# Image attention of a four-layer Flamingo kernel: output products in odd steps, the gathered keys' exponentials on ScalarE, routing's sends in every second step

## The chip, the core and the metric

The program runs on one core of one Trainium2 chip. The metric is the device time of one execution in microseconds (us), lower is better. Engines are called by the profile's names: PE is TensorE (its weight loads are PEld), DVE is VectorE, ACT is ScalarE, POOL is GpSimd, SP is the queue that issues the hardware DMAs.

## What is computed

Four layers work on `x` (4 batches of 512 tokens, 128 wide). Each adds a gated cross-attention and a gated feed-forward block. The change touches the first attention and the first steps of the routing that follows it. Cut to that, the reference is:

```python
def _L0_xattn_ref(image_embeds, latents, ln1_g, ln1_b, ln2_g, ln2_b, Wq, Wkv, Wo):
    x = layer_norm(image_embeds, ln1_g, ln1_b)       # ctx_1024: 4 x 154 x 128
    l = layer_norm(latents, ln2_g, ln2_b)            # layernorm(x): 4 x 512 x 128
    q = l @ Wq
    kv = jnp.concatenate([x, l], axis=1) @ Wkv       # 666 keys
    k, v = jnp.split(kv, 2, axis=-1)                 # 16 heads of 64
    w = softmax(q k^T / 8)                           # 4 x 16 x 512 x 666
    out = w @ v
    return out @ Wo

def _L0_ffn_ref(x, gate_w, gate_b, expert_bias, w1, b1, w2, b2):
    top_idx = jnp.argmax(x @ gate_w.T + gate_b + expert_bias, axis=-1)   # 8 experts
    ...

x = x + tanh(g_xattn[0]) * _L0_xattn_ref(ctx_1024, _layernorm(x), ...)
x = x + tanh(g_ffn[0]) * _L0_ffn_ref(_layernorm(x), ...)
```

## The kernel before

Every engine has its own program, written out by hand, and waits on semaphores where it needs another. Nothing is scheduled by a tool: the order in which an engine's function issues is the order in which it runs. The first attention (`image_pe`, `image_ve`, `image_ac`, `image_po`, `image_sp`) is a loop of 271 steps `i` that all engines walk through. The first 256 each start one piece of 128 queries of one head with all 666 keys. Four of them make a unit (two heads, two query tiles), two units a group (a pair of heads), and eight groups (64 steps) a batch.

What one step `i` issues, with the lines that the trace shows:

- **PE**: scores of step `i` (four products, L715) into one of two pairs of PSUM banks; in even steps a part of the product with the values of the unit before last (L749, 18 or 12 products, and in one of the two also L755 and the transposes L647); the transposes of the probabilities of step `i-2` (four on L726 into bank 4, the fifth on L730 into bank 5); where `i % 4 == 3` one more transpose of `rest` (L733); then, in even steps, a part of the projections of the next group (L495) into bank 7, called `side`.
- **DVE**: the maximum of step `i` over 666 scores (L787); in odd steps the low half of the projection of the step before (L860, L868, or L872 and L875, by part), which frees bank 7; the copy of the fifth tile out of bank 5 (L801); where `i % 4 == 3` also the product of a finished unit with its inverse sums (L783, at the step's start) and two instructions on `rest` (L808, L809), of which the second frees bank 5.
- **ACT**: the copy of the four transposed tiles of step `i-2` (L901), then the exponential of step `i` out of PSUM with its row sum (L911, 128x666, followed by the read of the accumulator), then every fourth step L920, and in even steps the high half of the projection (L943, L949, L955, L957).
- **POOL**: the low halves of the transposed probabilities of step `i-3` (two instructions on L1028); every fourth step L998 and L1006; and a copy of 32 columns (L1034, semaphore mark `gathered`): the last 32 of the 666 keys of step `i-1` go from `probs` into `rest`, where the four pieces of a unit stand side by side, to be transposed together by PE (L733). PE waits for the copies, and the exponential of step `i` waits for the copy of step `i-3`, because it overwrites that buffer. From step 32 on POOL also splits weights of the next layer in every fourth step (L1061, L1062, L1065).

Three things are placed by step numbers. `image_late` says in which steps PE multiplies a finished batch's `mixed` by `Wo`: four steps in a row, each with one tile of 128 tokens and 24 products of 128x128 (L495, `out<-in` named `banks<-weights_a,work`), followed by DVE's addition to `x` (L844). These products use bank 7 too (for the last batch banks 7 and 4), and wait until `mixed_low`, POOL's L1006, has passed the batch's last unit. `image_chores` says where the routing of the next layer starts: at step 222 its logits, at 225 its ranks, and from 227 on twelve `send`s, each an indirect DMA issued by POOL (L1185). `rest_due` says when `rest` is transposed.

The bank that PE takes is guarded by `bank`: it waits for the event that last freed it. For bank 7 in a late step that is DVE's low half of the projection issued one or more steps earlier; for a projection after a late product it is L844.

## Time and profile before

| what | value |
| --- | --- |
| time, median of 3 runs (lowest to highest) | 1881.87 us (1881.65 to 1882.85) |
| the profiled execution: its own time | 1886.16 us |
| the profiled execution: span | 1884.3 us |
| PE busy | 1471.7 us (78%) |
| DVE busy | 1181.1 us (63%) |
| ACT busy | 808.0 us (43%) |
| POOL busy | 780.4 us (41%) |
| chain that ended last, by engine | PE 52%, DVE 25%, ACT 7%, issue 7%, POOL 5%, DMA 3% |

The image attention lies between about 36 and 687 us of the span. The profiled execution took 4.3 us more than the median; the 1.9 us between its time and its span lie outside the traced program. A busy share is an average over the eight parts of the program, so what a step costs has to be read in the stretch in which it lies.

### The profile page before, as it was taken

The numbers are of one execution on the slowest core, as the hardware profiler recorded it, in microseconds if no ns is written. First come the engines' busy times: TensorE is split into PE (matmuls) and PEld (weight loads), VectorE is DVE, ScalarE is ACT, GpSimd is POOL, SyncE is SP. The second block draws the span as 40 slices with busy tenths as digits, with TensorE's granted clock in tenths as the row PEclk, the third lists the DMA queues.
The fourth block names the chain that finished last, engine by engine and source line by source line (L and its number), as shares of the span: only waits on it lengthen the run. The fifth ranks groups of instructions, "written<-read, shape, count | busy, mean of one in ns | idle before, by whom it ended". The sixth has DMA issues, their size and how long they took to land.

```text
span 1884.3 us, 32544 instructions
## 1 busy us (share of the span) xinstructions
PE 1471.7 (78%) x11363; PEld 955.5 (51%) x11485; DVE 1181.1 (63%) x3053; ACT 808.0 (43%) x1838; POOL 780.4 (41%) x1240
## 2 busy tenths in 40 slices
PE   4899899999989859463288689958966885578877
PEld 2666666667766648351265345523442333335444
DVE  4777577667766636438938656554566556776643
ACT  3777677767766626210044245533212542111011
POOL 4789798888767944400012333000002101243220
PEclk9999999999999989756568799979996977788887
DMA  6323222112112113300000000000000000000000
GB/s 246 90 80 108 67 71 53 43 39 54 45 42 54 50 47 101 115 0 0 1 0 1 11 5 1 2 1 1 1 1 1 1 1 1 0 1 6 5 2 11
DMA packets 35446, 63.96 MB, mean 34 GB/s; under 512 B 7527, under 2 KB 25026, under 8 KB 34131
## 3 DMA queue, kind: packets, MB, share of 16 engines
q1 hardware_dynamic: 33815, 59.77, 10.6%
q0 software_dynamic: 1472, 2.12, 0.3%
q8 instruction: 94, 1.54, 0.3%
q14 instruction: 65, 0.53, 0.1%
HBM read 30.59 MB, written 12.66 MB: 23 GB/s over the span
## 4 chain that ended last, share of the span: by engine, by line
PE 52%; DVE 25%; ACT 7%; issue 7%; POOL 5%; DMA 3%; SPq 0%; ACTq 0%; DVEq 0%; POOLq 0%
PE banks L495 13%; PE banks L715 4%; PE banks L749 4%; PE banks L1955 4%; PE banks L726 3%; ACT work L911 2%; DMA work<-work 2%; DVE xn L441 2%; PE banks L1941 2%; PE banks L1867 1%; PE banks L470 1%; DVE norm_room L405 1%; PE banks L1908 1%; POOL work L1028 1%; PE banks L2647 1%
## 5 line engine op out<-in xcount | busy, mean ns | idle before, releaser
L1028 POOL TENSOR_TENSOR work<-work 128x512 bf16<-128x512 f32 (+1 forms) x512 | 358.8, 724 | 96.4 <-ACT work L901 94.1
L435 POOL TENSOR_TENSOR norm_room<-norm_room,minus_half 128x4 f32<-128x4 f32 x48 | 50.1, 1045 | 537.3 <-DVE norm_room L410 535.4
L787 DVE TENSOR_REDUCE work<-banks 128x1 f32<-128x666 f32 x256 | 216.0, 844 | 50.8 <-PE banks L715 50.4
L911 ACT ACTIVATE work<-banks,work 128x666 f32<-128x666 f32 x256 | 209.1, 817 | 50.2 <-DVE work L787 42.7
L901 ACT ACTIVATE work<-banks 128x512 f32<-128x512 f32 x256 | 154.1, 602 | 131.4 <-PE banks L726 130.1
L715 PE MATMUL banks<-work 128*128 128x154 bf16 (+1 forms) x932 | 171.7, 299 | 28.2 <-DMA work<-work 17.9
L495 PE MATMUL banks<-work,weights_b 128*128 128x512 bf16 (+1 forms) x830 | 159.5, 350 | 12.6 <-DVE work L2282 5.1
L726 PE MATMUL banks<-const,work 128*128 128x128 f32 x1024 | 158.0, 277 | 2.2 <-ACT work L901 2.2
L715 PEld LDWEIGHTS banks<-work 128*128 128x128 bf16 x1024 | 91.7, 98 | 109.2 <-DMA work<-work 22.2
L476 ACT ACTIVATE xt<-banks 128x512 f32<-128x512 f32 x48 | 28.7, 598 | 264.0 <-PE banks L470 264.0
L470 PE MATMUL banks<-const,xn 128*128 128x128 f32 x176 | 39.8, 367 | 130.4 <-DVE xn L441 84.0
L749 PE MATMUL banks<-work 128*64 128x256 bf16 x1920 | 133.8, 279 | 7.1 <-POOL work L1028 5.3
L2032 DVE TENSOR_REDUCE work<-banks 128x2 f32<-128x308 f32 x192 | 86.6, 474 | 72.0 <-PE banks L1913 39.3
L495 PEld LDWEIGHTS banks<-work,weights_b 128*128 128x128 bf16 (+1 forms) x840 | 83.7, 101 | 84.4 <-issue 20.5
L2854 POOL TENSOR_TENSOR work<-work 128x512 bf16<-128x512 f32 x64 | 67.6, 1060 | 139.4 <-DVE work L2803 139.4
L726 PEld LDWEIGHTS banks<-const,work 128*128 128x128 f32 x1024 | 111.9, 141 | 16.6 <-issue 15.1
L749 PEld LDWEIGHTS banks<-work 128*64 128x64 bf16 x1920 | 97.3, 108 | 24.8 <-POOL work L1028 8.0
L2011 ACT ACTIVATE work<-banks 128x256 f32<-128x256 f32 (+1 forms) x256 | 85.6, 382 | 56.2 <-PE banks L1944 36.2
L470 PEld LDWEIGHTS banks<-const,xn 128*128 128x128 f32 x176 | 26.2, 184 | 143.4 <-DVE xn L441 77.8
L801 DVE COPY work<-banks 128x128 f32<-128x128 f32 x256 | 72.3, 282 | 39.2 <-PE banks L730 37.9
L730 PE MATMUL banks<-const,work 128*128 128x128 f32 x256 | 73.1, 285 | 8.1 <-ACT xt L478 2.9
L1941 PE MATMUL banks<-work 128*128 128x256 bf16 (+1 forms) x256 | 64.7, 287 | 14.6 <-ACT work L2003 11.6
(416 smaller groups left out, 3317.0 us busy)
## 6 DMA issues: line engine op xcount, KB each, us to landing
work<-work SPq DMA_DIRECT2D x128, 166.5 KB, 3.0
sorted<-in_pads SPq DMA_DIRECT2D x10, 838.5 KB
weights_b<-in_weights SPq DMA_DIRECT2D x1, 4120.0 KB, 23.9
work<-scratch SPq DMA_DIRECT2D x64, 64.0 KB, 2.0
weights_b<-in_weights SPq DMA_DIRECT2D x1, 2824.0 KB, 9.6
weights_a<-in_weights SPq DMA_DIRECT2D x1, 2056.0 KB, 9.1
weights_a<-in_weights SPq DMA_DIRECT2D x1, 2050.0 KB, 10.0
work<-work SPq DMA_DIRECT2D x32, 64.0 KB, 1.9
```

What stands on the lines that cost most here:

```text
L470: i = pe.transpose(ps[:, j * P:j * P + rows], src[0:rows, j, :], self.eye[0:rows, 0:rows])
L495: m = pe.matmul(out, left(a), right(b), start=start and n == 0, stop=stop and n == 2)
L715: m = pe.matmul(slot[:, a:z], lhs, k[:, h, part, a:z], start=part == 0, stop=part == 1)
L726: m = pe.transpose(ps[:, t * P:(t + 1) * P], prob[:, t * P:(t + 1) * P], self.eye)
L749: pe.matmul(self.out_bank[64 * h:64 * h + 64, 0:2 * P], self.v[n % 3][:, t, of_values, 64 * h:64 * h + 64], self.probs_parts[u % 2][:, h, ...
L787: ve.tensor_reduce(self.neg_max[i % 4], self.slot[i % 2][:, 0:KEYS0], AX_X, ALU.max, negate=True).then_inc(self.mark("max"))
L901: ac.activation(self.probs_t[u % 2][:, h, 0:4, j * P:(j + 1) * P], self.bank_a.rearrange("p (t n) -> p t n", t=4), ACT.Copy).then_inc(self ...
L911: ac.activation(self.probs[i % 3], self.slot[i % 2][:, 0:KEYS0], ACT.Exp, bias=self.neg_max[i % 4], accum_out=self.sums[u % 4][:, 2 * j + ...
L1028: po.tensor_tensor(parts[:, :, :, 0], exact, parts[:, :, :, 1], ALU.subtract).then_inc(self.mark(event, i - 3))
L1941: m = pe.matmul(bank, left, a.q4[b % 2][:, g, cols], start=True, stop=s != 4)
L2011: ac.activation(out, self.bank_of(k, HALF)[0:rows_n, :], ACT.Exp).then_inc(self.mark("exp4", s, n))
L2032: ve.tensor_reduce(a.most[u % 2][:, c % 2, 2 * g:2 * g + 2], self.bank_of(n % 3, 2 * CTX).rearrange("p (h k) -> p h k", h=2), AX_X, ALU.ma ...
```

## The change

Three edits, all within the first attention:

1. `image_late`: the four products with `Wo` of a batch stood in steps 73, 74, 75, 76 (and 64, 128, 192 later). They now stand in 69, 71, 73, 75. The first two wait for one unit less of `mixed_low`.
2. `gathered` is gone. POOL no longer copies 32 columns per step; instead ACT computes the exponentials of these 32 scores a second time, straight from PSUM into `rest`, ahead of the exponential of all 666. The wait of the exponential on the copy goes too, and PE's transpose of `rest` waits for `exp`.
3. `send`s stand in steps 227, 229, ..., 249 in place of 227 to 238.

```diff
-        elif 5 <= route < 5 + ROUTED:
-            out.append(("send", route - 5, 0))
+        elif route in range(5, 5 + 2 * ROUTED, 2):
+            out.append(("send", (route - 5) // 2, 0))
...
-        late = i - 8 * PAIRS - 9
-        if late >= 0 and late % (8 * PAIRS) < QT:
-            return late // (8 * PAIRS), late % (8 * PAIRS)
+        late = i - 8 * PAIRS - 5
+        if late >= 0 and late % (8 * PAIRS) in range(0, 2 * QT, 2):
+            return late // (8 * PAIRS), late % (8 * PAIRS) // 2
...
-                pe.wait_ge(*self.at("mixed_low", 2 * PAIRS * (b + 1)))
+                pe.wait_ge(*self.at("mixed_low", 2 * PAIRS * (b + 1) - int(t < 2)))
...
-            pe.wait_ge(*self.at("gathered", 4 * rest + 3))
+            pe.wait_ge(*self.at("exp", 4 * rest + 4))
...
-                    ac.wait_ge(*self.at("gathered", i - 3))
...
+                at = 32 * (2 * j + h)
+                ac.activation(self.rest[u % 2][:, at:at + 32], self.slot[i % 2][:, KEYS0 - 32:KEYS0], ACT.Exp, bias=self.neg_max[i % 4])
...
-            if 1 <= i < SUBS + 1:
-                u, _, _, _, h, j = self.image_sub(i - 1)
-                if (h, j) == (0, 0) and u >= 2:
-                    po.wait_ge(*self.at("turned_b", 4 * u - 2))
-                po.wait_ge(*self.at("exp", i))
-                po.tensor_copy(self.rest[u % 2][:, 32 * (2 * j + h):32 * (2 * j + h + 1)], self.probs[(i - 1) % 3][:, KEYS0 - 32:]).then_inc(self.mark("gathered", i - 1))
```

**On PE, the first batch's second late product, before** (step 74; `x24` on `weights_a,work` is the product with `Wo`, L715 the scores, L749 the values, L726 and L730 the transposes). It comes right behind the transposes of its own step, and a projection follows it:

```order
L715 MATMUL banks<-work 128x512 x2
L715 MATMUL banks<-work 128x154 x2
L749 MATMUL banks<-work 64x256 x12
L755 MATMUL banks<-work 128x128 x6
L647 MATMUL banks<-const,work 128x128 x2
L726 MATMUL banks<-const,work 128x128 x4
L730 MATMUL banks<-const,work 128x128
L495 MATMUL banks<-weights_a,work 128x128 x24
L495 MATMUL banks<-weights_c,weights_a 128x512 x2
L495 MATMUL banks<-weights_c 128x512
```

**The same product now** (step 71), with the end of step 70 ahead of it:

```order
L495 MATMUL banks<-weights_a,weights_c 128x128 x2
L495 MATMUL banks<-weights_c 128x128
L495 MATMUL banks<-weights_a,weights_c 128x128
L715 MATMUL banks<-work 128x512 x2
L715 MATMUL banks<-work 128x154 x2
L726 MATMUL banks<-const,work 128x128 x4
L730 MATMUL banks<-const,work 128x128
L733 MATMUL banks<-const,work 128x128
L495 MATMUL banks<-weights_a,work 128x128 x24
```

Between the projection of step 70 and the late product of step 71 PE now has only one short step: its scores and six transposes. No projection follows within the step.

**On ACT, one step now** (L901 the copy of step `i-2`, L911 the new exponential, L912 the old one; L921 and L950 are L920 and L949 of before):

```order
L901 ACTIVATE work<-banks 128x4x128
L911 ACTIVATE work<-banks,work 128x32
L912 ACTIVATE work<-banks,work 128x666
L921 ACTIVATE work<-banks 128x256
L950 ACTIVATE work<-banks 128x512
```

The 128x32 row is new in every step, between the copy and the exponential.

**On POOL, from the copy that ends step 226 to the transposed tiles of step 228, before** (L1185 is the send, L1034 the copy of 32 columns):

```order
L1034 COPY work<-work 128x32
L1185 DMA sorted<-xn,places 16640x129
L1028 TENSOR_TENSOR work<-work 128x4x128
L1028 TENSOR_TENSOR work<-work 128x128
L1034 COPY work<-work 128x32
L998 COPY work<-work 128x256
L1006 TENSOR_TENSOR work<-work 128x256
L1185 DMA sorted<-xn,places 16640x129
L1028 TENSOR_TENSOR work<-work 128x4x128
L1028 TENSOR_TENSOR work<-work 128x128
```

**The same place now**, from the send of step 227 to that of step 229 (the send is L1180, L1029 is L1028 of before, L999 and L1007 are L998 and L1006):

```order
L1180 DMA sorted<-xn,places 16640x129
L1029 TENSOR_TENSOR work<-work 128x4x128
L1029 TENSOR_TENSOR work<-work 128x128
L999 COPY work<-work 128x256
L1007 TENSOR_TENSOR work<-work 128x256
L1029 TENSOR_TENSOR work<-work 128x4x128
L1029 TENSOR_TENSOR work<-work 128x128
L1180 DMA sorted<-xn,places 16640x129
```

Two steps' work stands between two sends, and the copies are gone.

## Rows read from the trace of the kernel before

**Rows 1.** Busy time by stretch: us from:to, length, busy (x instructions) by engine, PEclk, DMA.

```profile
453.19:470.95 17.76, 17.50 (x179) 13.03 (x181) 12.89 (x31) 14.05 (x35) 14.15 (x29) 1.00 0.20 52
293.51:313.45 19.94, 17.90 (x179) 12.99 (x181) 14.97 (x39) 14.24 (x35) 18.76 (x34) 1.00 0.18 45
```

**Rows 2.** Timeline of one unit: start us, us, engine, line, what [idle before <-releaser].

```profile
455.57 0.60 PE L726 MATMUL banks<-const,work 128*128 128x128 f32 x4
...
456.27 0.60 ACT L901 ACTIVATE work<-banks 128x512 f32<-128x512 f32 x1 [1.18 <-PE banks L726]
...
456.76 0.81 ACT L911 ACTIVATE work<-banks,work 128x666 f32<-128x666 f32 x1
...
457.56 0.38 ACT L920 ACTIVATE work<-banks 128x256 f32<-128x256 f32 x1
...
457.97 0.42 DVE L783 TENSOR_TENSOR work<-banks,work 128x256 f32<-128x256 f32 x1 [1.29 <-ACT work L920]
457.99 0.73 PE L715 MATMUL banks<-work 128*128 128x512 bf16 x4
...
458.31 0.84 DVE L787 TENSOR_REDUCE work<-banks 128x1 f32<-128x666 f32 x1
...
459.07 0.68 DVE L872 TENSOR_TENSOR work<-banks,work 128x512 bf16<-128x512 f32 x1
...
460.18 0.30 DVE L809 TENSOR_TENSOR work<-banks,work 128x128 bf16<-128x128 f32 x1
...
460.54 0.33 PE L730 MATMUL banks<-const,work 128*128 128x128 f32 x1
```

**Rows 3.** Waits of PE's weight loads, 36 to 687 us: us in total, times, longest us.

```profile
PEld banks L730 <- DVE work L809: 13.4, 42, 0.4
```

**Rows 4.** ACT's short exponentials, groups by shape (1700 to 1884 us): busy us, mean ns | idle.

```profile
L2721 ACT ACTIVATE work<-banks,work 128x512 f32<-128x512 f32 x3 | 2.1, 687 | 5.9 <-DVE work L2825 5.9
...
L2721 ACT ACTIVATE work<-banks,work 128x128 f32<-128x128 f32 x3 | 1.1, 368 | 8.2 <-DVE work L2825 8.2
```

**Rows 5.** PE's waits around the late products of the third batch, 505 to 547 us.

```profile
PE banks L495 <- DVE x L844: 1.2, 2, 0.8
PE banks L495 <- DVE scratch L868: 1.1, 1, 1.1
PE banks L715 <- DMA work<-work: 1.1, 1, 1.1
PE banks L495 <- DVE work L872: 1.0, 1, 1.0
```

**Rows 6.** Timeline behind a part-2 projection, where step 69 now has its late product.

```profile
462.36 0.73 PE L715 MATMUL banks<-work 128*128 128x512 bf16 x4
...
463.32 0.80 DVE L875 TENSOR_TENSOR work<-banks,work 122x128 bf16<-122x128 f32 x3
```

**Rows 7.** PE's waits for POOL where the sends stand, 599 to 641 us.

```profile
PE banks L749 <- POOL work L1028: 5.3, 2, 2.9
```

**Rows 8.** Busy time by stretch, right behind the longer of these two waits.

```profile
635.00:640.00 5.00, 5.00 (x35) 3.47 (x36) 0.62 (x2) 1.88 (x4) 5.00 (x11) 0.66 0.00 0
```

**Rows 9.** Timeline of POOL between two sends.

```profile
606.30 1.00 POOL L1185 DMA_INDIRECT sorted<-xn,places  x1 [0.17 <-ACT work L911]
...
607.33 1.41 POOL L1028 TENSOR_TENSOR work<-work 128x512 bf16<-128x512 f32 x2
...
608.66 0.21 POOL L1034 COPY work<-work 128x32 f32<-128x32 f32 x1
...
609.04 1.00 POOL L1185 DMA_INDIRECT sorted<-xn,places  x1 [0.17 <-issue]
```

**Rows 10.** Timeline of the tail, where the last batch's late products stand.

```profile
677.05 1.92 PE L749 MATMUL banks<-work 128*64 128x256 bf16 x30 [0.98 <-DVE work L783]
...
680.66 0.61 POOL L1006 TENSOR_TENSOR work<-work 128x256 bf16<-128x256 f32 x1 [3.06 <-DVE work L783]
681.33 5.68 PE L495 MATMUL banks<-weights_a,work 128*128 128x128 bf16 x96 [1.69 <-POOL work L1006]
```

**Rows 11.** ACT's waits, 36 to 687 us.

```profile
ACT work L911 <- POOL work L1006: 2.6, 7, 0.4
ACT work L911 <- POOL work L1028: 1.8, 5, 0.4
ACT work L911 <- POOL work L1034: 1.1, 3, 0.6
```

More of the change, by code:

```diff
@@ L190 @@
         "clear": "filled", "tokens": "filled", "four_times": "filled", "wo_low": "filled", "mixed_low": "low_b", "summed": "router_steps", "ranked": "routed",
-        "places": "placed", "tile_stats": "ve", "gathered": "low_b", "padded": "router_steps", "relative": "router_steps", "delta": "router_steps",
+        "places": "placed", "tile_stats": "ve", "padded": "router_steps", "relative": "router_steps", "delta": "router_steps",
         "mix": "router_steps", "gates": "gate_steps", "gate_exp": "gate_steps"}
```

## The prediction

> **What bounds the kernel now.** All three edits lie in the first attention (36 to 687 us), so I read that stretch alone, in this order: busy time by stretch, to find the engine that is full; the timeline of one unit of four steps, to see what is waited for; PE's waits by releaser, to see how often; then the three places where the steps are moved.
>
> In an undisturbed group (eight steps) PE is busy for 17.50 of 17.76 us [rows 1]. That reads as "PE is the bound", but the timeline shows how thin this is. The reader should follow one unit from PE's transposes of an even step: they start at 455.57 and are issued by 456.01 (four, 0.11 us apart). ACT copies them from 456.27, starts the exponential at 456.76, and L920 at 457.56; DVE multiplies with that from 457.97, takes the next maximum at 458.31, the low half of the projection at 459.07, and then L809 at 460.18, which frees bank 5. PE's fifth transpose waits for it and starts at 460.54 [rows 2]. PE had issued the four transposes ahead of it by about 460.23, so it lost some 0.3 us. This loop is closed once per unit, from transposes to transposes, and it ends last: PE's weight load on L730 waits for L809 in 42 of 64 units, 13.4 us in all [rows 3]. So PE and a chain ACT, DVE, PE run level, with the chain 0.3 us behind. Whatever lengthens that chain is paid in full; ACT's and POOL's shares (14.05 and 14.15 of 17.76 us, rows 1) say nothing on it. **The exponential stands in the chain, POOL doesn't.**
>
> **The change part by part.**
>
> *The second exponential on ACT.* 256 instructions of 128x32 are added, each between the copy (L901) and the exponential (L911), so in each unit one of them is in the chain. No row shows this shape. The nearest are exponentials out of PSUM with a bias from SBUF, as this one: 128x512 takes 687 ns, 128x128 takes 368 ns [rows 4], so 0.83 ns a column, and 32 columns would take 0.29 us. Instructions of ACT overlap: the copy of 0.60 us starts at 456.27 and the exponential behind it at 456.76 [rows 2], 0.11 us before its end. So each new one delays the next by 0.29 - 0.11 = 0.18 us. The bounds: 0.29 if it doesn't overlap; below, 0.06, if the bias cost nothing and the fixed part were hidden; nothing at all if the chain weren't the bound (a rival). I take 0.18. How often: all 64 units close the chain or a longer one that holds the exponential too (through the projection's copies, the DMA of the keys and the next scores); I leave out four for the start, so 60 x 0.18 = **+10.8 us**, with 3.6 and 17.4 as ends.
>
> The Trainium skill (ScalarE: Activation LUTs, section "What ACT_TABLE_LOAD costs") states 280 ns + 0.833 ns a column for an ACTIVATE with a pointer as bias, and an overlap of 93 ns between neighbours. By it the new instruction would take an estimated 307 ns and delay the next by 0.21 us, and the change's sum would be 1.8 us higher; for the two shapes in rows 4 it gives 0.71 and 0.39 us where the trace has 0.687 and 0.368, so I stay with the rows.
>
> *The copies taken from POOL.* 256 x 0.21 us [rows 9] go. Outside the sends nothing waits for POOL except in name (see the rivals), so they bring nothing there; the work that remains (L1028) is what PE needs, two steps after it is ready. Counted with the sends below.
>
> *The products with Wo.* The 24 products themselves are unchanged, four times in each batch. What changes is the wait for bank 7. Before, in each of the first three batches, PE waits 1.1 us for L868 and 1.0 us for L872 ahead of the odd ones (73, 75), and 1.2 us in two waits for L844, since a projection stands right behind the even ones; the third batch also shows 1.1 us for the DMA of the keys at the start of the group ahead [rows 5], and so does the first (same row, 190 to 232 us), but not the second. Now each product stands in an odd step, one short step behind the projection of the even step whose low half has to free the bank:
> - steps 71 and 75 (`i % 4 == 3`): the chain above up to the end of L872 is 459.07 + 0.68 = 459.75, with 0.1 us to PE 459.85. PE would be ready when it starts the next scores, at 457.99 [rows 2]. That is 1.86 us each, and since the chain starts at the transposes of the step before, the stall of an earlier late product doesn't shorten it.
> - step 69: L875 ends at 464.12 and PE is ready at 462.36 [rows 6], so 1.86 us with the same 0.1.
> - step 73: as before, 1.1 us [rows 5].
>
> Sum 6.7 us against 3.3, or 4.4 with the DMA wait, which the stalls at 69 and 71 now cover. In the second batch one wait of 0.3 us for L809 goes too. So +2.3, +3.1 and +2.3: **+7.7 us**. As bounds I take 0 (as many stalls as before) and +10 (the DMA waits stay).
>
> *The sends.* One costs POOL 1.00 us and 0.17 ahead of it, and from one to the next it takes 609.04 - 606.30 = 2.74 us [rows 9], against 2.22 us per step elsewhere (17.76 / 8, rows 1). Over 12 steps POOL falls behind until PE waits for L1028, 5.3 us in two waits [rows 7]; behind the longer one PE's granted clock is 0.66 over 5 us [rows 8], between its levels of 1.2 and 2.4 GHz, which I put at 0.34 x 5 = 1.7 us. Now 24 steps hold the sends: eight steps of POOL cost 14.15 - 8 x 0.21 + 4 x 1.17 = 17.2 us, less than the 17.8 to 18.1 that the others take. So both go, less 0.6 us for what the chain would take anyway: **-6.4 us**. Ends: -3 and -8.
>
> *The tail.* The last batch's 96 products start at 681.33, when L1006 (680.66) is done, and take 5.68 us; PE had been idle for 1.69 us [rows 10]. Two of the four may now start before the last unit is finished: one between L749's 18 and 12 products of 677.05, one behind its transposes. They fill the idle time and leave some 0.4 us of waiting for L1006: **-1.3 us**. Ends: -2 and 0.
>
> The sum is 10.8 + 7.7 - 6.4 - 1.3 = **+10.8 us**. The profiled execution would go from 1886.16 us (span 1884.3) to 1897.0, and the median of the runs, 4.3 us below it, from 1881.87 to **1892.7 us**, 0.57% slower.
>
> **The rivals.**
>
> *POOL sets the pace in the groups with weight splits; the change is faster.* In such a group POOL is busy for 18.76 of 19.94 us and the group takes 2.2 us longer than the undisturbed one [rows 1], and the trace names POOL as what released 15 exponentials, 5.5 us in all [rows 11]. If the copies on POOL held such a group up, 8 x 0.21 = 1.7 us of each would go. There are 16 groups with splits (steps 32 to 160); I take half of them to be like the one shown, -13 us, with the exponential paid only in the others (+5.4) and the moved steps cancelling (+7.7 - 7.7): -8 in all, 1874 us (1860 if all 16 gain). It decides for faster once the gain over all groups passes 9.2 us, 0.6 us for each of the 16. For it: the two rows. Against it: PE's waits name POOL in the sends alone, and at most of those releases ACT's own copy had ended only just before, so the copy on POOL is a tie rather than the cause. Chance 0.14.
>
> *The odd steps cost nothing.* If DVE's low halves come earlier than in the undisturbed group, the waits of the late products stay as they are and the sum is 10.8 - 7.7 = +3.1: 1885 us, within 0.2% or just over. For it: before, the waits ahead of 73 and 75 are only 1.1 and 1.0 us. Against: 75 profits there from the late product of 74, which lay in the chain's shadow and no longer does. Chance 0.15.
>
> *The chain has room.* If PE's own 17.50 us are the bound, the second exponential disappears in the 0.3 us: 7.7 - 7.7 = 0, 1882 us. Rows 3 speak against it: a wait that shows in 42 units is no room. Chance 0.12.
>
> *The sends still hold POOL up*, now over 24 steps, because it waits for ACT's copies in between: +10.8 + 6.4 = +17, 1899 us. Chance 0.07. My forecast has the remaining 0.52.
>
> **How the numbers follow.** About 0.2% (3.8 us) is what a measurement of this kernel can tell from no change. Slower by more: the forecast and the last rival, most of the half in which sizes differ, and a third of the "odd steps" case: 0.65. Within: most of "odd steps" and of "the chain has room": 0.19. Faster: the POOL case and the rest: 0.16. The range: 1892.7 with the ends of the exponential (-7, +7) and of the late products (-8, +2) gives 1880 to 1901; to leave out no more than 2 in 10 I go to 1879 and 1902, which takes in the rivals but the first. The forecast's own range is 1886 to 1901.
>
> **What would show it.** In the new profile: the 128x32 rows at about 0.29 us and the main exponential starting 0.18 us after them; an undisturbed group of 18.1 us in place of 17.76; PE's waits on L730 longer than 0.3 us, about 0.5; four waits of PE before each batch's products with Wo, three near 1.9 us and one of 1.1, and none for L844; no wait of PE for L1028 (now L1029) between steps 227 and 250, and a granted clock of 1.0 there; no idle time ahead of the last products. I am wrong if groups keep 17.76 us, or if groups with splits get shorter.

## The result, and the profile after

| | before | changed |
| --- | --- | --- |
| median of 4 runs (lowest to highest), us | 1882.36 (1881.65 to 1887.31) | 1915.45 (1908.32 to 1917.57) |
| the profiled execution, time and span, us | 1886.16, 1884.3 | 1917.49, 1915.7 |

The changed kernel is slower, ratio 1.0158 (95% interval 1.013 to 1.0186). The forecast was 1892.7 us with a range of 1879 to 1902: right in sign, a third of the size. Of the 31.4 us between the two profiled spans, 22.2 lie in the image attention (its last addition L844 ends at 687.40 before, 709.63 now), 9.2 in what follows.

The page of the changed kernel, engine totals and two groups (L911 is now the new exponential, L912 the old one; the lines from there to POOL's L1029, which is L1028 of before, are one further):

```profile
PE 1504.4 (79%) x11485; PEld 966.0 (50%) x11485; DVE 1187.1 (62%) x3053; ACT 851.0 (44%) x2094; POOL 742.7 (39%) x984
...
L749 PE MATMUL banks<-work 128*64 128x256 bf16 x1920 | 136.7, 282 | 2.1 <-DVE work L783 1.8
...
L730 PE MATMUL banks<-const,work 128*128 128x128 f32 x256 | 72.7, 284 | 13.4 <-DVE work L809 7.4
```

ACT gained 256 instructions (2094, before 1838), POOL lost 256 (984, before 1240), and the waits on POOL ahead of L749 [rows 7] are gone. Busy time by stretch: first the undisturbed group, then the group with splits of rows 1 and steps 225 to 249, in which the sends stand.

```profile
472.87:491.22 18.35, 18.02 (x182) 13.01 (x181) 12.95 (x31) 15.45 (x42) 12.95 (x21) 1.00 0.20 51
```

```profile
304.67:324.51 19.84, 17.99 (x182) 13.02 (x181) 14.79 (x40) 15.65 (x42) 17.15 (x26) 1.00 0.18 46
622.24:679.46 57.22, 53.63 (x549) 38.92 (x547) 40.03 (x98) 45.59 (x123) 50.32 (x72) 1.00 0.23 61
```

The undisturbed group takes 18.35 us where it took 17.76 [rows 1]; the one with splits 19.84 against 19.94, so the prediction's last sign of being wrong, a shorter group with splits, shows in this one (e10 and e11 below take it up). ACT's groups by shape, over the attention:

```profile
L912 ACT ACTIVATE work<-banks,work 128x666 f32<-128x666 f32 x256 | 209.7, 819 | 0.0
...
L911 ACT ACTIVATE work<-banks,work 128x32 f32<-128x32 f32 x256 | 73.9, 289 | 47.5 <-DVE work L787 46.9
```

One unit of the undisturbed group, the same instructions as in rows 2, and what follows them up to the next unit's transposes:

```profile
475.36 0.60 PE L726 MATMUL banks<-const,work 128*128 128x128 f32 x4
...
476.06 0.60 ACT L901 ACTIVATE work<-banks 128x512 f32<-128x512 f32 x1 [0.94 <-PE banks L726]
...
476.55 0.28 ACT L911 ACTIVATE work<-banks,work 128x32 f32<-128x32 f32 x1
...
476.72 0.82 ACT L912 ACTIVATE work<-banks,work 128x666 f32<-128x666 f32 x1
...
477.51 0.39 ACT L921 ACTIVATE work<-banks 128x256 f32<-128x256 f32 x1
...
477.94 0.42 DVE L783 TENSOR_TENSOR work<-banks,work 128x256 f32<-128x256 f32 x1 [1.47 <-ACT work L921]
```

```profile
480.15 0.31 DVE L809 TENSOR_TENSOR work<-banks,work 128x128 bf16<-128x128 f32 x1
480.36 0.84 DVE L787 TENSOR_REDUCE work<-banks 128x1 f32<-128x666 f32 x1
...
480.51 0.33 PE L730 MATMUL banks<-const,work 128*128 128x128 f32 x1 [0.19 <-DVE work L809]
...
481.31 0.29 ACT L911 ACTIVATE work<-banks,work 128x32 f32<-128x32 f32 x1 [0.30 <-DVE work L787]
481.50 0.81 ACT L912 ACTIVATE work<-banks,work 128x666 f32<-128x666 f32 x1
...
482.45 0.54 PEld L715 LDWEIGHTS banks<-work 128*128 128x128 bf16 x4 [0.19 <-ACT work L912]
482.45 0.74 PE L715 MATMUL banks<-work 128*128 128x512 bf16 x4
...
484.50 0.49 PE L726 MATMUL banks<-const,work 128*128 128x128 f32 x3
```

The same two places of before, behind its L730 at 460.54 (its next scores start at 462.36 [rows 6], and no wait for ACT stands ahead of them):

```profile
461.35 0.82 ACT L911 ACTIVATE work<-banks,work 128x666 f32<-128x666 f32 x1 [0.21 <-DVE work L787]
...
464.40 0.49 PE L726 MATMUL banks<-const,work 128*128 128x128 f32 x3
```

The reader should see two passages through the new exponential, not one. From L726 to L730 it is 480.51 - 475.36 = 5.15 us, before 460.54 - 455.57 = 4.97 [rows 2]: that is the chain of the prediction, +0.18. But from L730 on there is a second one: DVE's maximum, the new exponential (481.31), the old one (481.50, ends 482.31), and only then the bank is free for the scores at 482.45. That part, up to the next unit's L726, takes 3.99 us; before it was 464.40 - 460.54 = 3.86, so +0.13. Over the whole attention PE's weight loads of the scores wait for the exponential 31 times where they waited 13 times (first before, then the changed kernel: us in total, times, longest):

```profile
PEld banks L715 <- ACT work L911: 6.1, 13, 0.7
```

```profile
PEld banks L715 <- ACT work L912: 10.5, 31, 0.9
```

PE's waits in the 16 steps of the third batch's late products:

```profile
PE banks L495 <- DVE work L872: 1.9, 1, 1.9
PE banks L495 <- DVE work L875: 1.9, 1, 1.9
PE banks L495 <- DVE work L860: 1.9, 1, 1.9
PE banks L495 <- DVE scratch L868: 1.2, 1, 1.2
```

That is as forecast. What was not forecast stands in the last number but two, the granted clock, of busy time by stretch (first batch, 2.5 us each):

```profile
203.38:205.88 2.50, 1.72 (x22) 1.24 (x19) 1.53 (x4) 2.15 (x9) 1.97 (x3) 1.00 0.00 0
205.88:208.38 2.50, 1.39 (x24) 1.42 (x25) 1.23 (x5) 1.50 (x4) 1.40 (x2) 0.98 0.39 91
208.38:210.88 2.50, 2.50 (x19) 1.38 (x16) 1.29 (x3) 0.00 (x0) 0.00 (x0) 0.50 1.23 354
210.88:213.38 2.50, 2.50 (x31) 2.17 (x27) 0.29 (x1) 0.75 (x3) 0.07 (x1) 0.83 0.43 178
```

The first of the four waits ends at 206.99. Within 1.5 us of it the clock is at 0.50, the lower of PE's levels (1.2 GHz), and stays there for some 3 us. It happens once more in this batch, behind the last of the four waits, which ends at 231.2. The 16 steps of each batch as a whole:

```profile
194.25:247.20 52.95, 44.59 (x458) 33.28 (x457) 28.84 (x70) 31.18 (x83) 31.18 (x46) 0.94 0.22 67
```

```profile
363.83:415.44 51.61, 43.11 (x458) 32.42 (x457) 28.82 (x70) 31.35 (x83) 31.23 (x46) 0.97 0.14 36
```

```profile
527.93:578.16 50.23, 42.98 (x458) 32.47 (x457) 28.71 (x70) 30.53 (x83) 25.98 (x41) 0.97 0.14 36
```

Before, these took 46.59, 45.76 and 45.41 us, at 1.00.

The clock also falls in places that the change did not make. At step 222, while PE runs the 24 thin products of the routing's logits (128x8), it goes to 0.50 for 3.4 or 6.8 us in 12 of the 17 profiles of this document, before (587.6) and changed (614.5) among them. Such a fall costs time in whichever profile happens to have it, so sums of profiles carry it as noise.

Last the tail, PE's timeline (rows 10 of before):

```profile
701.59 1.56 PE L495 MATMUL banks<-weights_a,work 128*128 128x128 bf16 x24
...
704.46 1.54 PE L495 MATMUL banks<-weights_a,work 128*128 128x128 bf16 x24
706.32 2.93 PE L495 MATMUL banks<-weights_a,work 128*128 128x128 bf16 x48 [0.31 <-POOL work L1007]
```

Two of the four products did move into the idle time ahead of L1007.

### The profile page after: what moved, and what is told of

Read it like the earlier page. It is cut to its first block, busy times and chain, and to the rows that moved or that the text cites. A ratio compares the mean times of both kernels' runs of the same rounds, so it can differ in the third digit from the quotient of the medians.

```text
span 1915.7 us, 32544 instructions
## 1 busy us (share of the span) xinstructions
PE 1504.4 (79%) x11485; PEld 966.0 (50%) x11485; DVE 1187.1 (62%) x3053; ACT 851.0 (44%) x2094; POOL 742.7 (39%) x984
## 4 chain that ended last, share of the span: by engine, by line
PE 52%; DVE 26%; ACT 10%; issue 6%; DMA 3%; POOL 2%; SPq 0%; ACTq 0%; DVEq 0%; POOLq 0%
PE banks L495 12%; ACT work L912 4%; PE banks L749 4%; PE banks L715 4%; PE banks L1950 4%; PE banks L726 3%; DMA work<-work 2%; DVE xn L441 2%; PE banks L1936 2%; PE banks L1862 2%; PE banks L470 1%; DVE work L787 1%; PE banks L1903 1%; DVE norm_room L405 1%; PE banks L755 1%
## 5 line engine op out<-in xcount | busy, mean ns | idle before, releaser
L1029 POOL TENSOR_TENSOR work<-work 128x512 bf16<-128x512 f32 (+1 forms) x512 | 357.7, 723 | 161.0 <-ACT work L901 159.4
L787 DVE TENSOR_REDUCE work<-banks 128x1 f32<-128x666 f32 x256 | 216.0, 844 | 45.5 <-PE banks L715 44.7
L912 ACT ACTIVATE work<-banks,work 128x666 f32<-128x666 f32 x256 | 209.7, 819 | 0.0
L901 ACT ACTIVATE work<-banks 128x512 f32<-128x512 f32 x256 | 155.0, 605 | 117.9 <-PE banks L726 112.6
L715 PE MATMUL banks<-work 128*128 128x512 bf16 (+1 forms) x1024 | 190.7, 309 | 20.3 <-DMA work<-work 12.8
L726 PE MATMUL banks<-const,work 128*128 128x128 f32 x1024 | 157.4, 276 | 2.4 <-ACT work L901 2.3
L715 PEld LDWEIGHTS banks<-work 128*128 128x128 bf16 x1024 | 90.3, 98 | 113.2 <-DMA work<-work 16.7
L749 PE MATMUL banks<-work 128*64 128x256 bf16 x1920 | 136.7, 282 | 2.1 <-DVE work L783 1.8
L726 PEld LDWEIGHTS banks<-const,work 128*128 128x128 f32 x1024 | 111.5, 141 | 16.7 <-issue 15.6
L749 PEld LDWEIGHTS banks<-work 128*64 128x64 bf16 x1920 | 100.3, 110 | 21.7 <-issue 6.5
L911 ACT ACTIVATE work<-banks,work 128x32 f32<-128x32 f32 x256 | 73.9, 289 | 47.5 <-DVE work L787 46.9
L730 PE MATMUL banks<-const,work 128*128 128x128 f32 x256 | 72.7, 284 | 13.4 <-DVE work L809 7.4
```

The lines of the kernel that those rows point to most:

```text
L715: m = pe.matmul(slot[:, a:z], lhs, k[:, h, part, a:z], start=part == 0, stop=part == 1)
L726: m = pe.transpose(ps[:, t * P:(t + 1) * P], prob[:, t * P:(t + 1) * P], self.eye)
L749: pe.matmul(self.out_bank[64 * h:64 * h + 64, 0:2 * P], self.v[n % 3][:, t, of_values, 64 * h:64 * h + 64], self.probs_parts[u % 2][:, h, ...
L787: ve.tensor_reduce(self.neg_max[i % 4], self.slot[i % 2][:, 0:KEYS0], AX_X, ALU.max, negate=True).then_inc(self.mark("max"))
L901: ac.activation(self.probs_t[u % 2][:, h, 0:4, j * P:(j + 1) * P], self.bank_a.rearrange("p (t n) -> p t n", t=4), ACT.Copy).then_inc(self ...
L912: ac.activation(self.probs[i % 3], self.slot[i % 2][:, 0:KEYS0], ACT.Exp, bias=self.neg_max[i % 4], accum_out=self.sums[u % 4][:, 2 * j + ...
```

## The experiments

The table gives what each profiled execution shows, in us: the length of stretches between the starts of DVE's maxima (L787) of two steps, the granted clock in parentheses where it isn't 1.00; the end of the attention; and the span behind it, where all kernels run the same code. Each run's ratio is to executions of before that were taken beside it; their medians lie between 1883.8 and 1890.0 us (1890.0 for e9 to e12), so times of different runs should be compared by their ratios.

| kernel | 65-81 | 129-145 | 193-209 | 161-193 | 225-249 | end | behind |
| --- | --- | --- | --- | --- | --- | --- | --- |
| before | 46.59 | 45.76 | 45.41 | 71.08 | 61.53 (0.97) | 687.40 | 1196.9 |
| changed | 52.95 (0.94) | 51.61 (0.97) | 50.23 (0.97) | 73.42 | 57.22 | 709.63 | 1206.1 |
| e5_after_again | 51.44 (0.97) | 49.99 | 50.21 (0.97) | 73.60 | 57.12 | 710.16 | 1196.4 |
| e1_exp_only | 47.47 | 46.60 | 45.97 | 73.48 | 60.52 (0.97) | 700.03 | 1201.1 |
| e9_exp_behind | 47.11 | 46.19 | 45.61 | 72.27 | 58.61 | 690.83 | 1210.5 |
| e10_exp_added | 47.50 | 46.66 | 46.52 | 73.42 | 61.59 (0.97) | 701.25 | 1204.5 |
| e11_no_copies | 46.76 | 45.64 | 45.24 | 71.02 | 61.19 (0.97) | 689.13 | 1206.6 |
| e2_late_odd_only | 48.57 | 48.72 | 47.43 | 71.06 | 62.81 (0.97) | 695.68 | 1190.5 |
| e14_odd_again | 48.62 | 48.61 | 47.44 | 71.07 | 60.03 (0.97) | 695.96 | 1201.9 |
| e6_exp_and_odd | 51.44 (0.97) | 53.05 (0.94) | 48.64 | 73.56 | 60.59 (0.97) | 711.89 | 1192.6 |
| e15_odd_exp_local | 51.27 (0.97) | 49.85 | 50.17 (0.97) | 71.04 | 61.64 (0.94) | 701.01 | 1197.2 |
| e13_behind_odd_sends | 49.14 | 49.35 | 47.92 | 72.28 | 56.29 | 695.80 | 1191.8 |
| e12_exp_two_odd | 47.68 | 47.77 | 47.97 (0.96) | 73.42 | 58.94 | 700.62 | 1196.4 |
| e4_late_even_only | 44.30 | 44.37 | 43.11 | 71.06 | 62.55 | 681.73 | 1204.9 |
| e7_exp_and_even | 44.97 | 44.99 | 43.69 | 73.42 | 60.32 (0.97) | 693.50 | 1196.8 |
| e3_sends_only | 46.71 | 45.74 | 45.45 | 71.05 | 55.84 | 680.91 | 1196.7 |
| e8_even_and_sends | 44.32 | 44.23 | 43.07 | 71.06 | 55.55 | 674.21 | 1204.9 |

The last column spreads from 1190.5 to 1210.5 us, and between two executions of the changed kernel by 9.7 us. So the edits are weighed by where the attention ends, and the times of the runs stand beside them. Each row is one profiled execution.

### Each edit alone

**e1_exp_only**: the second exponential, POOL's copies gone (cut, against before).

```diff
-                    ac.wait_ge(*self.at("gathered", i - 3))
+                ac.activation(self.rest[u % 2][:, at:at + 32], self.slot[i % 2][:, KEYS0 - 32:KEYS0], ACT.Exp, bias=self.neg_max[i % 4])
```

> Only the second exponential on ACT in place of POOL's copy; late products and sends stand as before. Theory A (two passes): each unit of four steps holds the added 0.17 us twice, once ahead of L783 and once ahead of the next scores, so an undisturbed group goes from 17.77 to 18.36 us and the attention ends about 17 to 19 us later than before, less 1 us because POOL is a little lighter in the sends: 1898 to 1901 us if what comes after the attention keeps its time. Theory B (one pass, as forecast): 18.1 us a group, +10.8, 1893 us. Theory C (the loss of the changed kernel needs the parts together): under +5 us here.

1900.81 us, ratio 1.0076 (1.0049 to 1.0103). The attention ends 12.6 us later. Theory A is right for undisturbed groups (steps 161 to 193 are four of them, 73.48 / 4 = 18.37 us) and too high in the sum (17 to 19 us): elsewhere a unit pays less.

**e2_late_odd_only**: the four products in odd steps (the `image_late` edit and the wait on one unit less).

> Only the products with Wo moved to odd steps. Theory A: PE waits three times 1.7 us (1.9 less the 0.17 of the added exponential) and once 1.1 us ahead of them in each batch, and its granted clock falls below 1.0 right behind some of them, as in the changed kernel (0.83 and 0.72 over 5 us); 16 steps (65 to 81) take 3.5 to 5 us more than before in each of three batches, the tail gains 1.3 us: +10 to +12 us, 1892 to 1894 us. Theory B (waits alone, as forecast): +7.7 - 1.3, 1888 us. Theory C (the odd steps cost nothing): under +2 us.

1889.12 us, ratio 1.002 (0.9997 to 1.0043); the attention ends 8.3 us later, at a full clock in the three batches. Theory A missed: the waits are 1.7, 1.7, 1.1 and 1.7 us as it said, but no fall stands behind them.

**e3_sends_only**: the `send` edit.

> Only the sends in every second step; POOL keeps its 32-column copies. Theory A: PE's waits for L1028 (5.3 us) go and the clock stays at 1.0 between 590 and 660 us, -6 us, 1876 us; POOL needs 14.15 + 4 x 1.17 = 18.8 us for eight steps that take 17.8, so it falls behind by 1 us a group and its slack of some 3 us just holds. Theory B (POOL without the copies removed is still too slow): a wait of PE for L1028 remains near step 249, -2 to -4 us.

1879.82 us, ratio 0.9986 (0.9956 to 1.0016): too small for the runs to tell, but the attention ends 6.5 us earlier. Of these, 5.7 lie in steps 225 to 249; 0.8 lie in steps 209 to 225, where this profile happens to have no fall of the clock at step 222.

The three alone sum to 12.6 + 8.3 - 6.5 = 14.4 us. Together they cost 22.2. So 7.8 us belong to no edit alone.

**e4_late_even_only**: even steps in place of odd (against e2_late_odd_only).

```diff
-        late = i - 8 * PAIRS - 5
+        late = i - 8 * PAIRS - 6
```

> Only the products with Wo moved, to even steps (70, 72, 74, 76 and 64, 128, 192 later), ahead of the projection of the same step. Theory A: what makes an odd step dear is that PE reaches bank 7 only one short step behind the projection, while in an even step two steps have passed and the product fills the time of the chain: no wait for DVE's low halves, only four waits of 0.5 to 0.8 us for L844; 16 steps take 0.5 to 2 us less than before in each of three batches, the tail gains about 1 us: 1876 to 1880 us. Theory B (every spread costs, since it stalls four steps in place of a run of four): +3 us or more, as the odd steps do.

1882.63 us, ratio 0.9984 (0.9962 to 1.0005); the attention ends 5.7 us *earlier* than before. At these products and the projections behind them PE waits for L844 alone, four times in a batch, 0.5 to 0.8 us each. What costs is the odd step, one step behind the projection, not the earlier place or the distance.

### What only the combination costs

> The changed kernel once more, on the chip that runs the next three. Its first attention ended at 709.6 us in the first profile, where the sum of the three edits made alone gives 687.4 + 12.6 + 8.3 - 6.5 = 701.8. Theory A (the 7.8 us are an interaction of the edits): it ends at 709 to 710 again, and steps 65 to 81 take 52.5 to 53.5 us again. Theory B (the 7.8 us were this one execution): it ends near 702, steps 65 to 81 take near 50 us. What comes behind the attention is the same code in both kernels; if the 9 us by which it was longer than before belong to the change, it takes 1204 us or more again, if they are the spread of runs, anything from 1190 to 1206.

1910.41 us, ratio 1.0153 (1.013 to 1.0176). The attention ends at 710.16, so a loss beyond the sum comes back, 8.3 us, but it isn't the same one. Against the sum of the three edits made alone, the three times 16 steps hold 7.6 us of it in the first profile and only 4.5 here, where the clock falls in two of three batches and steps 65 to 81 take 51.44 us, between the two theories. Another 3.0 us of e5's lie in steps 209 to 225, where the fall at step 222 lasts 6.8 us; kernels without the combination show that as well (e7, e11, e14), and e1 and e3 have no fall there, which makes the sum too low. What follows the attention takes 1196.4 us here, as before the change.

**e6_exp_and_odd** (sends as before) and **e7_exp_and_even**:

> The second exponential and the products with Wo in odd steps, the sends as before. Theory A (the interaction is between these two: only both together lower TensorE's granted clock in the 16 steps of the late products): the attention ends at 709.6 + 6.5 = 716, steps 65 to 81 take about 53 us, granted clock there below 1.00. Theory B (they only add): 687.4 + 12.6 + 8.3 = 708.3, steps 65 to 81 take 46.6 + 0.9 + 2.0 = 49.5 us at a granted clock of 1.00.

> The second exponential, with the products with Wo in the four even steps 6, 8, 10, 12 behind the group's start (that alone ended the attention 5.7 us earlier than before) in place of the odd ones; sends as before. Theory A (the clock falls in the long waits ahead of the odd products, four of 1.1 to 1.9 us in 8 steps, once the exponential is there too): with even steps these waits are short, the edits add, the attention ends at 687.4 + 12.6 - 5.7 = 694 (693 to 696), clock 1.00 in steps 65 to 81. Theory B (the second exponential makes late products cost more wherever they stand): 700 or later.

e6: 1917.62 us, ratio 1.0188 (1.0164 to 1.0211), attention ends at 711.9: above the plain sum of 708.3, below the 716 of theory A. e7: 1894.21 us, ratio 1.0073 (1.0046 to 1.01), 693.5 us, and full clock in the three batches: the exponential and even products simply add (687.4 + 12.6 - 5.7 = 694.3). So the extra cost lies between the exponential and the *odd* products. It doesn't need the sends: e6 has it in the three times 16 steps, 6.1 us beyond the sum, though less in the whole attention (3.6), since its steps 81 to 129 and 225 to 249 are some 1.5 and 1.2 us shorter than the sum.

It has two parts. Where the clock held, both edits together made the 16 steps 49.99 (e5) and 48.64 us (e6) long, against 49.56 and 47.99 by adding e1's and e2's gains to before: 0.4 and 0.7 us, some 1.6 us over three batches, if the first is as long at full clock as the second. The rest is the clock: each 0.03 below 1.00 goes with about 1.5 us more (50.21 against 48.64, 51.61 against 49.99), and the profiled changed kernel has four such falls, some 6 us.

**e12_exp_two_odd**: two of the four in odd steps, two in even ones (offsets 5, 7, 10, 12).

> The second exponential, with two of the four products in odd steps (5 and 7 behind the group's start) and two in even ones (10 and 12); sends as before. Theory A (TensorE's granted clock falls behind the row of four long waits ahead of the odd products): with two such waits it stays 1.00 in the 16 steps of all three batches, which then take the mean of the even version (44.97, 44.99, 43.69) and of the odd one at full clock (49.99, 49.99, 48.64): 47.5, 47.5 and 46.2 us, within 0.7 each. Theory B (any odd product beside the exponential can lower it): at least one of the three shows a clock of 0.97 and takes 1.5 us more.

1899.66 us, ratio 1.007 (1.0033 to 1.0107). Theory A fell: in the third batch the clock goes to 0.50 at 532.05, right behind the first wait of 1.9 us, which ends at 531.09. It takes no row of four waits. In the changed kernel, e5 and e6, too, each fall begins within 1.4 us behind one single wait of 1.9 us, the first, second or last of a batch, never behind that of 1.2.

Three runs ask what about the waits does it. **e13_behind_odd_sends** is the whole change with the second exponential behind ACT's back copy (the edit of e9, below); **e14_odd_again** repeats e2; **e15_odd_exp_local** adds to e2's edit the exponential in the late products' steps only, with POOL's copies kept:

```diff
+                if i >= 64 and i % 64 < 14:
+                    at = 32 * (2 * j + h)
+                    ac.activation(self.rest[u % 2][:, at:at + 32], self.slot[i % 2][:, KEYS0 - 32:KEYS0], ACT.Exp, bias=self.neg_max[i % 4])
```

> The whole change, with one difference: the second exponential stands behind the back copy of its step. Theory A (the clock falls behind waits of 1.9 us ahead of the odd products; with the exponential out of the chain they are 1.7 us, as without it, and the clock holds): 1.00 in the 16 steps of all three batches, which take 48.6 to 49.3, 48.6 to 49.3 and 47.4 to 48 us; the attention ends at 687.4 + 3.4 + 8.3 - 6.5 = 692.6 (692 to 695), 17 us ahead of the changed kernel. Theory B (the second exponential lowers the clock by its presence): a clock of 0.97 or less in at least one of the three batches, as in 7 of the 9 batches seen with the exponential and the odd products; the attention ends at 695 or later.

> The products in odd steps alone, once more: do they hold the clock, or was that luck in the three batches seen? Theory A: waits of 1.7 us, clock 1.00 in all three batches again, 48.6, 48.7 and 47.4 us. Theory B (odd products lower the clock now and then with or without the exponential): 0.97 or less in one or more of them, 1.5 us longer each.

> The products in odd steps, and the second exponential only in steps 0 to 13 of batches 2 to 4 (beside POOL's copies, which are kept), so 42 of them instead of 256. Theory A (what lowers the clock is the length of the waits there): waits of 1.9, 1.9, 1.2 and 1.9 us, clock at 0.97 or less in at least one of the three batches, those 16 steps at 49.0 to 53 us; everywhere else the times of the odd products alone (155.2, 114.8, 37.9, 71.1 us). Theory B (it takes the exponential in all steps): 1.00 in all three batches, 49.4, 49.4 and 48.0 us.

PE's waits in steps 65 to 81 of e13, and that stretch:

```profile
PE banks L495 <- DVE work L875: 1.9, 1, 1.9
PE banks L495 <- DVE work L872: 1.7, 1, 1.7
PE banks L495 <- DVE work L860: 1.7, 1, 1.7
PE banks L495 <- DVE scratch L868: 1.2, 1, 1.2
```

```profile
192.22:241.36 49.14, 41.35 (x458) 31.42 (x457) 28.83 (x71) 31.24 (x82) 31.59 (x47) 1.00 0.24 72
```

And the same of e15, with three waits of 1.9 and one of 1.2:

```profile
191.16:242.43 51.27, 43.06 (x458) 32.39 (x457) 28.81 (x70) 30.85 (x80) 33.66 (x63) 0.97 0.22 69
```

e13: 1894.05 us, ratio 1.006 (1.0035 to 1.0086), clock 1.00 in all three batches. The attention ends at 695.8 us, 13.8 us ahead of the changed kernel, but 3.2 us later than the sum I had expected, and at the end that theory B had named (695 or later). By the clock theory A is borne out, and the 3.2 us don't lie at the late products: the three times 16 steps are within 0.4 us of the sum, while steps 209 to 249 hold 3.0. There e9 and e3 had each made steps 225 to 249 shorter (58.61 and 55.84 us against 61.53), and together they can't gain that twice (56.29). e14: 1885.97 us, ratio 1.0017 (0.999 to 1.0043), full clock and the same lengths. e15: 1903.56 us (two executions), ratio 1.0101 (1.0039 to 1.0163), with the clock down in two of three batches although the exponential is there in 42 steps only; up to step 193 the other stretches are those of e2.

The single waits ahead of odd products, counted over all runs:

| waits | where | clock fell behind |
| --- | --- | --- |
| 1.9 us, 45 of them | changed, e5, e6, e15: nine each; e12: six; e13: three | 12 |
| 1.7 us, 24 of them | e2, e14: nine each; e13: six | 0 |

If the two kinds were alike, all 12 falls would land among the 45 by chance in 0.3% of cases. With even products (e4, e7, e8), whose waits are at most 0.8 us, the clock held in all 9 batches. So the falls go with the long waits, about one in four, and what the exponential does in them is to make the wait 0.2 us longer.

How far the length alone decides is less sure. Only e13 has the exponential in these steps and shorter waits: six of 1.7 us and three of 1.9, none with a fall. If each of the nine were as prone as the 42 other waits of 1.9 us (12 falls), none would fall in 5% of cases. And the place in the row counts too: 7 of the 12 falls stand behind the last wait of a batch (12 such waits), 5 behind the 33 others. Why, no run shows.

### Where the exponential is paid

**e9_exp_behind**: the second exponential issued behind the back copy (L920) and the bank freed by it (cut, against before).

```diff
-        slot = self.bank(pe, 2 * (i % 2), "exp", i + 1, n=2)
+        slot = self.bank(pe, 2 * (i % 2), "gathered", i, n=2)
...
                 ac.activation(out, self.out_bank[:, 2 * P:4 * P], ACT.Copy).then_inc(self.mark("spread_kept"))
+            if i < SUBS:
+                u, _, _, _, h, j = self.image_sub(i)
+                at = 32 * (2 * j + h)
+                ac.activation(self.rest[u % 2][:, at:at + 32], self.slot[i % 2][:, KEYS0 - 32:KEYS0], ACT.Exp, bias=self.neg_max[i % 4]).then_inc(self.mark("gathered", i))
```

> The second exponential alone, but issued behind the back copy (L920) of its step in place of ahead of the main exponential; the bank of the scores is then freed by it. Theory A (the second exponential is paid at two places of a unit, 0.17 us between L901 and L921 and 0.13 us between L809 and the next scores): the first 0.17 go, steps 161 to 193 (8 units) take 73.5 - 1.4 = 72.1 us, and up to 73 if the bank is now freed later. Theory B (what costs is its length on ACT, wherever it stands): 73.5 as with the exponential ahead. Theory C (the later release of the bank decides): 74 to 75.

Its timeline, one unit (L919 is L920 of before, L923 the second exponential), and the group:

```profile
459.98 0.60 PE L726 MATMUL banks<-const,work 128*128 128x128 f32 x4
...
461.97 0.39 ACT L919 ACTIVATE work<-banks 128x256 f32<-128x256 f32 x1
...
464.95 0.33 PE L730 MATMUL banks<-const,work 128*128 128x128 f32 x1
...
466.56 0.28 ACT L923 ACTIVATE work<-banks,work 128x32 f32<-128x32 f32 x1
...
466.90 0.55 PEld L715 LDWEIGHTS banks<-work 128*128 128x128 bf16 x4 [0.20 <-ACT work L923]
...
468.95 0.60 PE L726 MATMUL banks<-const,work 128*128 128x128 f32 x4
```

```profile
457.49:475.50 18.01, 17.91 (x182) 12.91 (x181) 12.94 (x31) 15.41 (x43) 12.97 (x21) 1.00 0.20 52
```

L726 to L730 is 4.97 us, exactly as before the change: the first passage is gone. L730 to the next L726 is 4.00, as in the changed kernel: the second is still paid, and here PE's weight load names the second exponential (L923) as what it waited for. Steps 161 to 193 take 72.27 us, within theory A (72.1 to 73), far from the 73.5 of B. The whole costs 3.4 us in the attention in place of 12.6, at the same ACT load (15.41 against 15.45 us per group). Part of that is the sends' stretch, where e9 happens to have no fall of the clock (58.61 us at 1.00, e1 60.52 at 0.97); without steps 209 to 249 it is 5.9 in place of 13.6. The runs take 1893.98 us, ratio 1.0013 (0.9978 to 1.0049).

**e10_exp_added** (before, plus the exponential, POOL's copies kept) and **e11_no_copies** (before, with the copies only in the first two units; the later units' last 32 keys are weighed with stale values) take the two halves of e1's edit apart (cut, e10's edit first):

```diff
+                at = 32 * (2 * j + h)
+                ac.activation(self.rest[u % 2][:, at:at + 32], self.slot[i % 2][:, KEYS0 - 32:KEYS0], ACT.Exp, bias=self.neg_max[i % 4])
...
-            if 1 <= i < SUBS + 1:
+            if 1 <= i < 9:
```

> The second exponential is added on ACT ahead of the main one, and POOL's copy is kept (it writes the same values over it). Theory A (POOL's copies cost nothing outside the sends): as the exponential without the copies, steps 0 to 225 end 12 to 13 us later than before, steps 161 to 193 take 73.5 us; only steps 225 to 249 get longer, to 62 to 63 us. Rival (taking the copies from POOL gave some of the exponential's price back in groups with splits): steps 0 to 161 take more than the 409.1 us of the exponential alone, by 3 us or more.

> The copy of the last 32 keys' exponentials is made only for the first two units and left out from then on (later units use stale values), with no second exponential: POOL's relief alone. Theory A: nothing outside the sends, steps 0 to 225 as before (558.9 to 559.2 us, first to last start), steps 225 to 249 shorter by 1 to 3 us. Rival (POOL sets the pace in groups with splits): steps 65 to 161 shorter than 244.3 us by 3 us or more.

e10: 1909.56 us, ratio 1.0099 (1.005 to 1.0147). Steps 0 to 225 end 13.5 us later than before, steps 0 to 161 take 408.4 us (409.1 in e1): no relief from POOL shows. In steps 225 to 249, 61.59, it missed: neither longer nor shorter than before. e11: 1891.23 us, ratio 1.0027 (1.0005 to 1.0049); steps 65 to 161 take 245.3 us against 244.3, the sends 61.19 against 61.53, less than I had expected. A single group can show otherwise. This is the group with splits of rows 1, in e10 and e11:

```profile
299.00:319.29 20.29, 18.02 (x182) 13.05 (x181) 14.73 (x39) 15.65 (x42) 18.55 (x34) 1.00 0.18 45
```

```profile
294.79:314.45 19.66, 17.86 (x182) 12.96 (x181) 15.03 (x39) 14.25 (x35) 17.38 (x26) 1.00 0.18 46
```

Here POOL's copies cost 0.3 to 0.5 us (19.94 to 19.66 without the exponential, 20.29 to 19.84 with it); over all groups nothing of it is left.

### A version that beats both

**e8_even_and_sends**: products in even steps, sends in every second step, the copy left on POOL.

> The version that I think beats both: products with Wo in even steps, sends in every second step, the copy left on POOL (no second exponential). If these two add: attention ends at 687.4 - 5.7 - 6.5 = 675 us; time of the kernel 12 us below before, about 1872, if what follows is as long as before. If the waits that both edits remove are shared: 679 to 681.

1877.57 us, ratio 0.996 (0.9943 to 0.9978). The attention ends at 674.2 us, 13.2 us ahead of before, a little better than the sum (675). The runs show half of that (medians 1877.57 and 1883.81); in the profiled one the time behind it is 8 us longer than in before's. Most of the missing half is a matter of the clock over the whole program: where it is 0.881 or 0.882, e8 takes 1870.1 to 1874.1 us (four executions), before 1877.6 to 1887.1 (nine, median 1882.9), 12 us apart. But eight of e8's twelve executions show 0.878 or less, and only two of the sixteen of before beside it (one of 7510 us left out).

## Why the prediction was wrong

**The late products: right.** Four waits ahead of the odd products, 1.9, 1.9, 1.9 and 1.2 us (forecast three of about 1.9 and one of 1.1), none for L844. The agreement of the 1.9 is in part luck: the 1.86 were worked out without the second exponential, and so measured the waits are 1.7 (e2, e14); the exponential adds the rest. Alone the products cost +2.0, +3.0 and +2.0 us in the three batches against +2.3, +3.1 and +2.3. The tail gave 1.1 us against 1.3. The rest of e2's 8.3 us is 1 us or so in steps 81 to 129 and 225 to 249 each, where runs of equal code differ by as much.

**The sends: right**, -6.5 against -6.4, or -5.7 in steps 225 to 249 alone; clock 1.00 there in the changed kernel, no wait for L1029. Beside the exponential they are worth less: from e1 to the changed kernel these steps go from 60.52 to 57.22.

**The exponential: the sum nearly right, by two errors.** 0.289 us and 0.17 behind its start are as forecast. The step that failed is "in each unit one of them is in the chain": in an undisturbed unit two are, and the group gets 0.59 us longer, not 0.36. Taking PE's wait at L730 as the only slack, I never followed the loop through the bank that the exponential frees. The other error is "all 64 units": steps 81 to 129 and 145 to 193, 24 units, pay 7.2 us (e1 against before), 0.30 each; the other 40 pay 5.5, some 0.14 each, and even that is after some 1.7 us which e1 gains in steps 209 to 249 (the sends' steps 1.0 shorter, no fall at step 222). Together 12.6 where I had 10.8. PE's wait on L730 grew from 0.32 to 0.42 us in the mean (13.4 us in 42 waits, 18.0 in 43), not to 0.5.

**The step that cost most is the sum itself.** The terms were added, 10.8 us, as if none changed another. Singly measured they are 14.4; together 22.2. Of the 7.8 us between, 7.6 lie in the three times 16 steps: about 1.6 are longer waits at full clock, some 6 the granted clock (four falls of some 1.5 us each). That term the prediction had put at nothing without a reason. Rows 8 had shown such a fall behind a long wait, of 2.9 us; I priced its disappearance among the sends and did not ask whether the new waits of 1.9 us would bring it back. That they do is shown by e15 against e2 and e14: the exponential in these steps alone brings the falls back. That it acts by the 0.2 us that it adds to the wait rests on e13, one profile.

**Behind the attention** the first profile shows 9.2 us more, in code that did not change, and the medians differ by more than the attention does (33.1 and 26.6 us in two measurements, the attention 22.2 and 22.8). e5, the same kernel, shows none in its profile. PE alone makes the difference: the whole stretch in before, changed and e5:

```profile
687.40:1884.30 1196.90, 865.38 (x5242) 505.09 (x5267) 716.09 (x1869) 346.39 (x763) 243.00 (x239) 0.81 0.04 12
```

```profile
709.63:1915.70 1206.07, 881.29 (x5267) 512.72 (x5267) 715.85 (x1869) 346.25 (x763) 243.08 (x239) 0.80 0.04 12
```

```profile
710.16:1906.60 1196.44, 865.83 (x5242) 505.93 (x5267) 715.87 (x1869) 346.11 (x763) 243.04 (x239) 0.81 0.04 12
```

DVE, ACT and POOL are busy as long in all three; PE is busy 16 us longer where the granted clock is lower. Before has such executions too, longer ones at a lower clock over the whole program. Whether the change makes them more frequent, or chance did, stays open: so a third of the 33.1 us of the first measurement is located and not explained.

**The ends of the range** are added up wrongly: -7 - 8 and +7 + 2 give 1877.7 to 1901.7 us, not 1880 to 1901. The stated range hardly changes by it.

**The rivals.** "POOL sets the pace" is refuted in sum by e10 and e11, though its mechanism is real in single groups. "The odd steps cost nothing" and "the chain has room" fell with the waits and the 0.59 us. "The sends still hold POOL up" fell with e3.

## What to carry to other kernels

An instruction added to an engine with idle time is priced by the loops it stands in: follow each loop once around, through every bank or buffer that the instruction helps to free, and count how often it is passed; the same instruction moved behind the copy that others wait for cost 3.4 us in place of 12.6 (5.9 for 13.6 without the steps in which the clock falls by chance). Where an edit adds waits of PE, look in the rows of before for a fall of the granted clock behind a comparable wait, and price the waits of all edits together, not one by one.

## What the runs showed of the hardware

PE's granted clock went from 1.00 to 0.50 behind 12 of 45 single waits of 1.9 us, in steps in which PE is busy for 44.59 of 52.95 us, and behind none of 24 of 1.7 us. So 0.2 us more of waiting went with a further 1.5 us, now and then. The places where it fell differed between two executions of the same kernel. The Trainium skill (TensorE: Matmul & The Clock Gate, section "A second HAM failure mode: psum-queue depth-cycling") says that PE's short idle times between groups of matmuls can be frequent enough for the clock to swing between its levels. The trace agrees that short idle times can do it, but how often they come isn't all that decides here: the even products stall PE as often, four times in a batch for 0.5 to 0.8 us, and show no fall.

Equal code behind the attention took 1190.5 to 1210.5 us, with lengths that recur: e4 and e8 agree within 0.1 us, and so do before, e3 and e7 (1196.7 to 1196.9). A change of 10 us can be lost or doubled in this if only one pair of spans is compared.
